# A gated expert stage and a per-sample step on one core: eight warm-up matmuls instead of six, and chunk 0's gate and up products ahead of chunk 1's

## What is computed

```python
# x: (16, 128, 128); side: (16, 8); share: (16,); step: (16,), 1..98
# Wg, Wu: (8, 128, 512), Wd: (8, 512, 128); Sg, Su: (128, 512), Sd: (512, 128); T: (100, 128, 128); all float32
g = einsum('bsd,edf->ebsf', x, Wg)
u = einsum('bsd,edf->ebsf', x, Wu)
expert_outs = einsum('ebsf,efd->ebsd', silu(g) * u, Wd)
expert = einsum('be,ebsd->bsd', side, expert_outs)
shared = (silu(x @ Sg) * (x @ Su)) @ Sd
x = x + (1 - share) * expert + share * shared
x = x + einsum('bij,bjk->bik', T[step - 1], x)
```

## Time and profile before

| | |
|---|---|
| median of 3 runs | 312.27 us (310.66, 312.27, 343.07) |
| the profiled execution | 310.24 us |
| its span, first to last instruction | 308.4 us |
| PE busy | 303.6 us, 98% of the span |
| DVE, ACT, POOL busy | 69%, 53%, 33% |

### The profile page before, as it was taken

The page is one execution under the profiler, slowest core; times in us unless marked ns, Lnnn a source line. Parts: engine busy times, 40 slices in busy tenths (PEclk is TensorE's granted clock), DMA queues, the critical chain, the costliest instruction groups (busy, mean ns, idle before and its releaser), DMA issues.

```text
span 308.4 us, 4555 instructions
## 1 busy us (share of the span) xinstructions
PE 303.6 (98%) x1356; PEld 251.2 (81%) x1356; DVE 213.9 (69%) x348; ACT 163.3 (53%) x303; POOL 102.3 (33%) x116
## 2 busy tenths in 40 slices
PE   7999999999999999999999999999999999999996
PEld 6788888888888888888888888888888888888884
DVE  2776677667776676667776677666776676667785
ACT  3765555555555555555555555555555555555552
POOL 3585114431144115511551144212441155180000
PEclk9999999999999999999999999999999999999999
DMA  7700300030003000120003000013000000000001
GB/s 196 256 2 0 103 1 2 0 102 1 0 0 102 0 0 0 25 77 0 0 0 118 19 24 26 26 28 99 0 0 0 0 0 0 0 2 0 34 36 68
DMA packets 9047, 10.39 MB, mean 34 GB/s; under 512 B 592, under 2 KB 8144, under 8 KB 9040
## 3 DMA queue, kind: packets, MB, share of 16 engines
q1 hardware_dynamic: 9040, 10.30, 10.8%
HBM read 9.25 MB, written 1.05 MB: 33 GB/s over the span
## 4 chain that ended last, share of the span: by engine, by line
PE 97%; DMA 1%; DVE 0%; SPq 0%; ACT 0%; issue 0%
PE o_bank L404 11%; PE o_bank L407 11%; PE o_bank L405 11%; PE g_bank L380 10%; PE u_bank L380 10%; PE g_bank L379 10%; PE u_bank L379 10%; PE g_bank L378 10%; PE u_bank L378 10%; DMA w_raw<-in_W_all 1%; PE o_bank L425 1%; PE o_bank L417 0%; DVE res L324 0%; PE u_bank L417 0%; PE g_bank L438 0%; PE g_bank L442 0%
## 5 line engine op out<-in xcount | busy, mean ns | idle before, releaser
L295 DVE TENSOR_TENSOR u_bank<-u_bank,silu_g 128x512 f32<-128x512 f32 x144 | 100.7, 699 | 85.9 <-PE u_bank L380 84.4
L238 ACT ACTIVATE silu_g<-g_bank 128x512 f32<-128x512 f32 x144 | 86.1, 598 | 133.9 <-PE g_bank L380 132.4
L301 DVE TENSOR_TENSOR h_lo<-u_bank,h_hi 128x512 fp32r<-128x512 f32 x144 | 97.9, 680 | 0.1
L220 POOL TENSOR_TENSOR acc<-acc,scaled 128x512 f32<-128x512 f32 x32 | 41.4, 1295 | 163.2 <-DVE scaled L309 163.1
L244 ACT ACTIVATE h_hi<-u_bank 128x512 fp32r<-128x512 f32 x144 | 85.4, 593 | 0.7 <-DVE u_bank L295 0.7
L404 PE MATMUL o_bank<-h_hi,w_hi 128*128 128x512 f32 x144 | 56.2, 391 | 0.0
L407 PE MATMUL o_bank<-h_lo,w_hi 128*128 128x512 f32 x144 | 56.1, 389 | 0.0
L405 PE MATMUL o_bank<-h_hi,w_lo 128*128 128x512 f32 x144 | 56.0, 389 | 0.0
L378 PE MATMUL g_bank<-x_hi,w_hi 128*128 128x512 f32 x142 | 55.6, 392 | 0.0
L379 PE MATMUL g_bank<-x_lo,w_hi 128*128 128x512 f32 x142 | 55.3, 389 | 0.0
L380 PE MATMUL g_bank<-x_hi,w_lo 128*128 128x512 f32 x142 | 55.3, 389 | 0.0
(11 more groups left out here) (51 smaller groups left out, 145.7 us busy)
## 6 DMA issues: line engine op xcount, KB each, us to landing
w_raw<-in_W_all SPq DMA_DIRECT2D x8, 768.0 KB, 4.5
T_plus<-in_TT SPq DMA_DIRECT2D x16, 64.0 KB, 1.7
out_y<-res SPq DMA_DIRECT2D x3, 256.0 KB, 2.5
acc<-in_xT SPq DMA_DIRECT2D x2, 256.0 KB, 3.6
w_raw<-in_W_all SPq DMA_DIRECT2D x2, 256.0 KB, 4.3
acc<-in_xT SPq DMA_DIRECT2D x1, 512.0 KB, 6.1
w_raw<-in_W_all SPq DMA_DIRECT2D x2, 128.0 KB, 3.0
out_y<-res SPq DMA_DIRECT2D x2, 128.0 KB, 2.4
```

The source lines that it names most:

```text
L220: nc.gpsimd.tensor_tensor(acc[:, t, :], acc[:, t, :], scaled[:, t % 2, :], ALU.add).then_inc(acc_done, 1)
L238: nc.scalar.activation(silu_g[:, k % 2, :], g_bank[k % 2][:, :], ACT.Silu).then_inc(g_read, 1)
L295: nc.vector.tensor_tensor(u_bank[k % HR][:, :], u_bank[k % HR][:, :], silu_g[:, k % 2, :], ALU.mult).then_inc(h_done, 1)
L301: nc.vector.tensor_tensor(h_lo[:, k % HR, :], u_bank[k % HR][:, :], h_hi[:, k % HR, :].bitcast(F32), ALU.subtract).then_inc(split_done, 1)
```

## The change

The warm-up has eight products instead of six. Before, PE took the first (high by high) part of gate and up of both chunks, and then the other two parts of chunk 0 and of chunk 1. Now it takes all three parts of chunk 0, each part for gate and up together and each behind its own signal, and only then turns to chunk 1: its gate in three matmuls, its up through the helper that the loop also uses. The same twelve matmuls are issued. No other engine's list is touched.

```diff
             pe.wait_ge(zero_done, 1)
-            warm_up(6)
-
-            def high(bank, c, m):
-                nc.tensor.matmul(bank, w_hi[:, 0, c, m, :], x_hi[:, 0, :], start=True, stop=False)
-
-            def low(bank, c, m):
-                nc.tensor.matmul(bank, w_hi[:, 0, c, m, :], x_lo[:, 0, :], start=False, stop=False)
-                return nc.tensor.matmul(bank, w_lo[:, 0, c, m, :], x_hi[:, 0, :], start=False, stop=True)
+            warm_up(8)
+
+            def opening(x_part, w_part, start, stop):
+                for bank, m in ((g_bank[0], 0), (u_bank[0], 1)):
+                    last = nc.tensor.matmul(bank[:, :], w_part[:, 0, 0, m, :], x_part[:, 0, :], start=start, stop=stop)
+                    if stop:
+                        last.then_inc(u_done if m else g_done, 1)
 
             pe.wait_ge(x_rounded, 1)
-            for c in range(2):
-                pe.wait_ge(w0_rounded, c + 1)
-                high(g_bank[c][:, :], c, 0)
-                high(u_bank[c][:, :], c, 1)
+            pe.wait_ge(w0_rounded, 1)
+            opening(x_hi, w_hi, True, False)
             pe.wait_ge(split_done, 1)
+            opening(x_lo, w_hi, False, False)
             pe.wait_ge(w_ready, 1)
-            low(g_bank[0][:, :], 0, 0).then_inc(g_done, 1)
-            low(u_bank[0][:, :], 0, 1).then_inc(u_done, 1)
+            opening(x_hi, w_lo, False, True)
+            pe.wait_ge(w0_rounded, 2)
+            nc.tensor.matmul(g_bank[1][:, :], w_hi[:, 0, 1, 0, :], x_hi[:, 0, :], start=True, stop=False)
+            nc.tensor.matmul(g_bank[1][:, :], w_hi[:, 0, 1, 0, :], x_lo[:, 0, :], start=False, stop=False)
             pe.wait_ge(split_done, 2)
-            low(g_bank[1][:, :], 1, 0).then_inc(g_done, 1)
-            low(u_bank[1][:, :], 1, 1).then_inc(u_done, 1)
+            nc.tensor.matmul(g_bank[1][:, :], w_lo[:, 0, 1, 0, :], x_hi[:, 0, :], start=False, stop=True).then_inc(g_done, 1)
+            project_u(1, 1)
```

## The result

The changed kernel has a median of 310.16 us (309.76 to 310.66, 20 runs), the kernel before, timed beside it, 310.57 us (20 runs). The ratio is 0.9971, 95% interval 0.9957 to 0.9985: a gain of 0.3%, 0.9 us by the ratio (0.5 to 1.3), small but clear of the noise. The profiled execution took 310.14 us with a span of 308.3 (before 310.24 and 308.4), so the two profiled executions show almost none of the gain.

| executions | n | above 311.4 us | median of the others |
|---|---|---|---|
| before | 20 | 7 | 310.38 |
| changed | 20 | 0 | 310.16 |

The account below looks back on a forecast made before the run. PE was taken to run without a wait from its first down product at 9.49 us, whose start POOL's last low part holds. The 0.74 us won is waited away, sum 0.00: forecast 310.7 us, range 309.6 to 313.0.

Parts of the forecast that it names:

- The sum of 0.00: Whole change: the 0.74 us PE wins in the opening is all waited away before the first down product.
- chunk 0's six matmuls: Opening on PE: a sign of being right, running from about 4.6 to 5.8 us without a hole.
- unit 2's gate: PE after both chunks' opening matmuls: a sign of being right, starting near 7.4 us.
- PE's wait of about 0.7 us: Before the first down product: PE idles from 8.78 to 9.49 us for POOL's last low part.
- Two strands, one start: First down product: starts when both PE's stream and the weights' work on ACT, DVE and POOL end, about 9.49 us.
- The clock: Opening: PE rises to 2.4 GHz at about 4.7 us as before; at most one real matmul slow, 0.2 us.
- Rival 2: Opening: longer warm-up and unbroken stream make the clock rise sooner or more surely; median 310.2 us; chance 0.10.
- Silu of unit 0: ACT, behind the gate's last matmul: moves forward by about 0.9 us from 6.95, giving nothing.
- POOL's rounding cover: Opening: POOL runs from 6.63 to 9.44 us without a gap, so ACT's down-weight rounding does not hold it.
- Rival 1: First down product: POOL does not hold it, so it starts at 8.78; 0.82 us less, 309.8; chance 0.10.
- Rival 3: Before the first down product: PE's 0.71 us hole lets the clock fall; +1.7 us, 312.4; chance 0.06.
- Rival 4: Opening: DVE's earlier make_h slows POOL's three low parts; +0.9 us, 311.6; chance 0.06.

Follow-up runs that it names:

- after_again: The changed kernel timed again without further edits, against the kernel before on the same chip: 310.33 us, ratio 0.9978, 0 of 12 late.
- w6_new_split: Changed kernel with six warm-up products instead of eight, and chunk 0's down weights rounded and split by themselves: 310.07 us, ratio 0.9966 to the kernel before.
- pool_late: Changed kernel plus one more 128x512 subtraction on POOL before its last low part of the opening: 311.22 us, ratio 1.0008 to the kernel before.
- copy_before: The kernel before, unchanged, timed again beside itself: 310.51 us, ratio 1.0002, 5 of 12 late.
- w6_new_again: Changed kernel with six warm-up products instead of eight, new order kept, timed a second time: 310.62 us, ratio 0.9980 to the kernel before, 1 of 12 late.
- hole_back: New order, six warm-up products, wait for chunk 1's weights put back behind the first two matmuls: 310.90 us, ratio 1.0005 to the kernel before, 6 of 12 late.

## Why the prediction was right, and where it was off

**The forecast** of 310.7 us without a change held in its range, which is 3.4 us wide and would have held a gain of twice the measured one. The sum of 0.00 held for executions in which the clock rises early: the first down product started at 9.43 against 9.49, the profiled times differ by 0.10 us, and in the second comparison (after_again) the executions below 311.4 us have the same median, 310.36 before and 310.33 changed. In the first they were 310.38 and 310.16; that 0.2 us is not explained further. The new median, 310.16, is 0.5 us below the forecast. That the start came out so near is in part luck. Of the signs that the prediction named, three came (16 warm-up records, line 404 at 9.43, a span of 308.3). Three did not: chunk 0's six matmuls reached to 6.40 instead of 5.8, unit 2's gate started at 8.00 instead of 7.4, and PE's wait of about 0.7 us shrank to 0.07.

**Two strands, one start:** right, and shown. An added 1.04 us on POOL moved the start by 1.03 and the median by 1.1; with the weights' strand shortened, PE's own bounded.

**Step "The clock": wrong.** "I take the same moment for the new kernel." There is no such moment. Among the profiled executions the rise lies before 4.43 us in w6_new_split, near 4.7 in the earlier trace rows, between 5 and 6.4 in eight others (5.9 in the changed kernel), near 7.1 with one warm-up product, 8.5 with four, and at 9.0 and 9.4 in the two late ones. The Trainium skill (TensorE: Matmul & The Clock Gate, section "What's actually happening") says that it varies from run to run; these runs agree. With it at 5.9 three real matmuls ran slow instead of at most one, and the slack of 0.71 us was 0.07.

**Rival 2** was what happened, and 0.10 was too little. The argument against it, "a hole of nearly the same size comes back at 8.78", failed twice: with the clock at 5.9 the hole was hardly there, and a hole behind the rise never showed a fall (pool_late idled 1.15 us at 9.3 and went on at 0.34 and 0.23). What the runs tie to late executions are holes ahead of the rise. The size was right in kind: I reckoned 8 matmuls at the lower level for 312.27 us, and the late execution of the before kernel had nine between 4.29 and 9.07. In the first comparison 5 of the 18 executions that count were late, by some 1.8 us each, which is 0.5 us in the mean; with the 0.2 us by which the others differ that is the 0.69 of the plain means. In the second, 12 of 29 by 1.5 us is 0.6 us.

**The terms.** First real matmul: 4.64 forecast, 4.50 measured. Silu of unit 0 was to move forward by 0.9 us and moved by 0.35 (6.95 to 6.60), and make_h started at 7.23, not 6.7, both by the later clock. POOL's rounding cover: I wrote that ACT's rounding of the down weights "was not what POOL waited for", as POOL ran without a gap. The kernel before has this row of ACT:

```profile
7.45 0.62 ACT L257 ACTIVATE w_hi<-w_raw 128x512 fp32r<-128x512 f32 x1
```

It ends at 8.07, and so does POOL's second low part (7.33 + 0.74), so the rows could not tell which of the two held the third part back. In the new kernel POOL did wait 0.41 us for ACT. That rounding could not move forward with silu, because its load came only then.

**The other rivals.** Rival 1 (no cover) fell with pool_late; its 309.8 should read 309.9, the forecast less 0.82. Rival 3 (a fall of the clock) had no hole to work on in the changed kernel, and fell with pool_late's longer one. Rival 4 (DVE slows POOL) fell: POOL's two low parts took 1.44 us, as before, with make_h now beside the second. In w6_new_split make_h, at 6.80, lay over the first, which took 0.74 us.

## What to carry to other kernels

When a kernel's executions fall into two groups, get a profile of each before costing a change: here most of the gain was in how often the slower group came up, and next to none in the profiled execution. Warm up until the real work surely arrives, and let nothing idle between. A wait behind the first two matmuls, with a warm-up that ends up to 0.3 us early, cost 1.5 to 2.0 us in four executions of ten. A warm-up of six products that ends 0.3 to 0.5 us early, with no wait behind, did so in 1 of 48. In front of a point where two strands meet within 0.1 us, shortening one of them wins nothing.

## What the runs showed of the hardware

The granted clock read 1.00 in stretches where matmuls of 512 columns were 0.43 us apart; the mean of an execution did not tell late ones from the others. A tile of zeros in the stream kept the early rise as well as real data did (0 of 12 late). A hole of 1.15 us behind the rise left the upper level as it was (pool_late). Why a hole of under 0.6 us in the opening costs up to 4 us more of the lower level in some executions (copy_before, w6_new_again) and nothing in others (hole_back, w6_new_split) is not settled by these runs; neither are the two executions of 343 us, which came only in the first session.
